# Expert outputs weighted per slot and scattered with an adding DMA into an output that already holds x1

## What is computed

```python
x = x + _L0_gnn_ref(_layernorm(x), ..., src, dst)                  # x1
x_flat = _layernorm(x)
gate_logits = x_flat @ Wg + bg + bias                              # 8 experts
topk_vals, topk_idx = jax.lax.top_k(gate_logits, 2)
topk_w = jax.nn.softmax(topk_vals, axis=-1)
combine = (one_hot(topk_idx, 8) * topk_w[..., None]).sum(axis=1)
h = relu(einsum('td,edh->teh', x_flat, W1) + b1)                   # 256 -> 512
y = einsum('teh,ehd->ted', h, W2) + b2                             # 512 -> 256
x = x + einsum('ted,te->td', y, combine)
```

## Time and profile before

| | us |
|---|---|
| timed runs, median of 3 | 2192.18 |
| lowest and highest | 2184.37, 2199.14 |
| the profiled execution's own time | 2198.43 |
| its span in the profile | 2196.7 |
| first `tick` of the expert loop | 1974.32 |
| last `tock` | 2160.16 |

### The profile page before, as it was taken

How to read it: one execution, slowest core, us unless ns; L and a number is a source line. 1 busy time by engine, 2 the same in 40 slices (tenths; PEclk the granted TensorE clock), 3 DMA queues, 4 the chain that set the end, 5 groups by cost and what they waited for, 6 DMA issues and landing times.

```text
span 2196.7 us, 31507 instructions
## 1 busy us (share of the span) xinstructions
PE 1910.3 (87%) x11090; PEld 1129.8 (51%) x11091; DVE 1117.5 (51%) x2548; ACT 594.1 (27%) x1268; POOL 304.1 (14%) x434
## 2 busy tenths in 40 slices
PE   1666767999999999999999999999999998649991
PEld 1533334445654456445654457444664455439991
DVE  7589992344524445244533445244533655635555
ACT  0145552112221223112222123121221111126660
POOL 0012224554000000000000000000000112123331
PEclk7779998999999999999999999999999999769996
DMA  9900004342000000000000000000000000633225
GB/s 272 336 10 0 0 0 154 133 141 93 1 2 1 1 1 2 1 1 1 1 2 1 1 1 1 1 1 1 1 1 1 20 20 32 284 112 85 78 85 193
DMA packets 74392, 113.64 MB, mean 52 GB/s; under 512 B 10634, under 2 KB 63669, under 8 KB 73232
## 3 DMA queue, kind: packets, MB, share of 16 engines
q1 hardware_dynamic: 56618, 52.49, 8.0%
q0 software_dynamic: 12736, 39.29, 5.2%
q10 hardware_dynamic: 4902, 20.01, 2.3%
HBM read 49.99 MB, written 61.77 MB: 51 GB/s over the span
## 4 chain that ended last, share of the span: by engine, by line
PE 67%; DVE 15%; issue 9%; POOL 5%; ACT 1%; SPq 1%; DMA 1%; ACTq 1%; DVEq 0%; POOLq 0%
PE bank L1401 35%; PE bank L1425 24%; DVE hot_key L759 6%; PE bank L1385 4%; POOL chosen_out L563 3%; DVE hot_row L753 2%; POOL slot_in L542 2%; PE bank L1380 1%; PE bank L1299 1%; SPq L435 1%; PE bank L1469 0%; DMA y_pair<-chosen_out 0%; PE bank L1327 0%; PE bank L1462 0%; DVE r_lo L819 0%
## 5 line engine op out<-in xcount | busy, mean ns | idle before, releaser
L1401 PE MATMUL bank<-adj,r_hi 128*128 128x512 fp8e4 (+2 forms) x2100 | 732.6, 353 | 0.0
L1401 PE MATMUL bank<-adj,r_lo 128*128 128x512 fp8e4 (+2 forms) x2100 | 732.2, 353 | 0.0
L1401 PEld LDWEIGHTS bank<-adj,r_hi 128*128 128x128 f16 x2100 | 206.4, 98 | 190.5 <-issue 2.0
L1401 PEld LDWEIGHTS bank<-adj,r_lo 128*128 128x128 f16 x2100 | 206.4, 98 | 190.5 <-issue 1.7
L826 DVE SCALAR_TENSOR_TENSOR m_lo<-bank,msg_unit,m_hi 128x512 f16<-128x512 f32 (+2 forms) x84 | 57.3, 683 | 302.3 <-ACT m_hi L1112 302.3
L1327 PE MATMUL bank<-hot_key,hot_row 128*128 128x400 f16 x588 | 138.9, 351 | 60.5 <-DVE hot_key L759 58.1
L1425 PE MATMUL bank<-x_hi,wht_hi 128*128 128x512 f16 (+2 forms) x504 | 178.0, 353 | 9.2 <-DVE gate_a L844 9.2
L1425 PE MATMUL bank<-x_lo,wht_hi 128*128 128x512 f16 (+2 forms) x504 | 178.0, 353 | 0.0
L1425 PE MATMUL bank<-x_hi,wht_lo 128*128 128x512 f16 (+2 forms) x504 | 178.0, 353 | 0.0
L1425 PE MATMUL bank<-m_hi,wct_hi 128*128 128x512 f16 (+2 forms) x504 | 177.8, 353 | 0.0
L1425 PE MATMUL bank<-m_lo,wct_hi 128*128 128x512 f16 (+2 forms) x504 | 177.7, 353 | 0.0
(11 more groups left out here) (279 smaller groups left out, 2893.4 us busy)
## 6 DMA issues: line engine op xcount, KB each, us to landing
slot_in<-fill_rows SPq DMA_DIRECT2D x2, 13520.0 KB, 69.4
ffn_scratch<-pair POOLq DMA_DIRECT2D x32, 512.0 KB, 3.2
ffn_w<-ffn_scratch ACTq DMA_DIRECT2D x8, 2048.0 KB, 16.0
x_rows<-in_L_ffn_W POOLq DMA_DIRECT2D x32, 256.0 KB, 4.0
slot_x<-slot_in SPq DMA_DIRECT2D x30, 260.0 KB, 2.8
y_pair<-chosen_out SPq DMA_DIRECT2D x8, 640.0 KB, 9.0
xa<-in_x SPq DMA_DIRECT2D x1, 3072.0 KB
x<-in_x ACTq DMA_DIRECT2D x1, 3072.0 KB
```

The costliest lines, as they stand in the source:

```text
L1401: last = mm(bank[f][:, 0:n], r[:, q, f * P:(f + 1) * P], c, start=q == 0 and i == 0, stop=q == NT - 1 and i == len(todo) - 1)
```

## The change

The weights are now applied in the expert loop, to each slot, and the scatter adds into `out` itself.

- The top logits' difference d travels with the row, in column `D + 2` of `x2_rows`, `slot_in` and `slot_x`. The work on `top` ahead of the loop is gone.
- ACT forms e^d per tile (`exp_now`) ahead of `xt_hi`; DVE keeps it in `meta` beside the two numbers.
- `output` writes the biased result into `y_sum`, makes `dest` (the node number alone), the weight `share`, and then `slot_y` in two multiplications. PE's `layer2` waits for `y_sum` only (`y_read`).
- The scatters go into `out` with `compute_op=ALU.add`; rows beyond the last node are out of bounds and left out.
- SP stores x1 into `out` window by window in the GNN's last step; GpSimd waits for these stores before the expert loop.
- The tail is gone.

```diff
@@ block.sync: in place of the wait for "rows"
-            sp.wait_ge(sem("rows"), rows_before(NW))
+            for w in range(NW):
+                t0, t1 = WIN_T0[w], WIN_T0[w] + WIN_TILES[w] - (w == NW - 1)
+                sp.wait_ge(sem("x1_sum"), rows_before(w + 1))
+                sp.dma_start(out[t0 * P:t1 * P, :].rearrange("(t p) d -> p t d", p=P), x1[:, t0:t1, :]).then_inc(sem("stored"), 16)
+            sp.dma_start(out[(NT - 1) * P:N, :], x1[0:TAIL, NT - 1, :]).then_inc(sem("stored"), 16)
             for e in range(NX):
                 sp.dma_start(out_bias[:, e, :], ...)
@@ block.sync: the end
             sp.wait_ge(sem("experts_done"), 1)
-            G = NT // FIN
-            for g in range(FIN):
...
-            for g in range(FIN):
-                t0, t1 = g * G, (g + 1) * G
-                sp.wait_ge(sem("summed"), t1)
...
-            sp.wait_ge(sem("stored"), 16 * (FIN + 1))
@@ block.gpsimd
+            pool.wait_ge(sem("stored"), 16 * (NW + 1))
             pool.wait_ge(sem("tiles_of"), 1)
...
-                    pool.wait_ge(sem("y_ready"), 2 * n + 4)
+                    pool.wait_ge(sem("y_ready"), n + 1)
                     pool.tensor_tensor(tick[:], valid[:], valid[:], ALU.mult).then_inc(sem("ticks"), 1)
                     for j in range(TT):
-                        pool.indirect_dma_start(chosen_out[:], bass.IndirectOffsetOnAxis(ap=dest[:, j:j + 1], axis=0),
-                                                slot_y[:, j, :], None).then_inc(sem("y_out"), 16)
+                        pool.indirect_dma_start(out[:], bass.IndirectOffsetOnAxis(ap=dest[:, j:j + 1], axis=0), slot_y[:, j, :], None,
+                                                bounds_check=N - 1, oob_is_err=False, compute_op=ALU.add).then_inc(sem("y_out"), 16)
@@ block.vector: choose
+                v.tensor_tensor(x2_rows[w % 2][:, 0:nt, D + 2], top[:, 1, t0:t0 + nt], top[:, 0, t0:t0 + nt], ALU.subtract)
@@ block.vector: before the loop
-            v.tensor_tensor(top[:, 2, :], top[:, 1, :], top[:, 0, :], ALU.subtract).then_inc(sem("top_diff"), 1)
-            dve.wait_ge(sem("top_exp"), 1)
...
@@ split_tile
-                v.tensor_copy(kept, slot_x[:, :, D:D + 2]).then_inc(sem("meta_kept"), 1)
+                v.tensor_copy(kept[:, :, 0:2], slot_x[:, :, D:D + 2])
+                v.tensor_copy(kept[:, :, 2], exp_now[:]).then_inc(sem("meta_kept"), 1)
@@ output
-                v.tensor_tensor(slot_y[:], bank[5][:]..., out_bias[:, e:e + 1, :]..., ALU.add)                 .then_inc(sem("y_ready"), 1)
+                v.tensor_tensor(y_sum[:], bank[5][:]..., out_bias[:, e:e + 1, :]..., ALU.add)\
+                 .then_inc(sem("y_read"), 1)
                 v.tensor_copy(meta_now[:], meta[:, bass.ds(n, 1), :, :]...).then_inc(sem("dest_part"), 1)
...
-                v.tensor_scalar(dest_f[:], meta_now[:, :, 1], float(e), float(NPAD), ALU.not_equal, ALU.mult).then_inc(sem("dest_part"), 1)
-                dve.wait_ge(sem("dest_part"), 2 * n + 2)
-                v.tensor_tensor(dest[:], dest_f[:], meta_now[:, :, 0], ALU.add).then_inc(sem("y_ready"), 1)
+                v.tensor_copy(dest[:], meta_now[:, :, 0])
+                v.tensor_scalar(total[:], meta_now[:, :, 2], 1.0, None, ALU.add).then_inc(sem("dest_part"), 1)
+                v.scalar_tensor_tensor(share[:], meta_now[:, :, 1], float(e), meta_now[:, :, 2], ALU.is_equal, ALU.max).then_inc(sem("dest_part"), 1)
+                dve.wait_ge(sem("dest_part"), DEST_OPS * n + 2)
+                v.reciprocal(total[:], total[:]).then_inc(sem("dest_part"), 1)
+                dve.wait_ge(sem("dest_part"), DEST_OPS * n + 4)
+                v.tensor_tensor(share[:], share[:], total[:], ALU.mult).then_inc(sem("dest_part"), 1)
+                dve.wait_ge(sem("dest_part"), DEST_OPS * n + 5)
+                dve.wait_ge(sem("y_read"), n + 2)
+                for j in range(TT):
+                    last = v.tensor_scalar(slot_y[:, j, :], y_sum[:, j, :], share[:, j:j + 1], None, ALU.mult)
+                last.then_inc(sem("y_ready"), 1)
@@ block.vector: the end
-            for t in range(NT):
...
-                v.scalar_tensor_tensor(x1[0:m, t, :], y_pair[0:m, t, 0, :], top[0:m, 0, t:t + 1], x1[0:m, t, :], ALU.mult, ALU.add).then_inc(sem("first_summed"), 1)
...
@@ block.scalar
-            act.wait_ge(sem("top_diff"), 1)
-            a.activation(top[:, 2, :], top[:, 2, :], ACT.Exp).then_inc(sem("top_exp"), 1)
 
             def tile_hi(n):
                 act.wait_ge(sem("turned"), n + 2)
+                a.activation(exp_now[:], slot_x[:, :, D + 2], ACT.Exp)
                 a.activation(xt_hi[:]..., bank[4][:], ACT.Copy).then_inc(sem("tile_hi"), 1)
@@ block.tensor
             def layer2(e, n):
-                pe.wait_ge(sem("y_ready"), 2 * n + 2)
+                pe.wait_ge(sem("y_read"), n + 1)
```

More of the change, by code:

```diff
@@ L68 @@
 TT = TILE // P
+DEST_OPS = 5
 CAP = (N + TILE - 1) // TILE * TILE
@@ L232, in gnn_ffn @@
         x2_rows = [lb(f"x2_rows{i}", [P, 4, ROW], F32) for i in range(2)]
-        top = lb("top", [P, 4, NT], F32)
+        top = lb("top", [P, 2, NT], F32)
         mv2 = lb("mv2", [P, NT, 2], F32)
@@ L282, in gnn_ffn @@
         xt_lo = fb("xt_lo", [P, DT, TILE], F32R)
-        meta = fb("meta", [P, MAX_TILES + 2, TT, 2], F32)
-        meta_now = fb("meta_now", [P, TT, 2], F32)
-        dest_f = fb("dest_f", [P, TT], F32)
+        meta = fb("meta", [P, MAX_TILES + 2, TT, 3], F32)
+        meta_now = fb("meta_now", [P, TT, 3], F32)
+        exp_now = fb("exp_now", [P, TT], F32)
+        total = fb("total", [P, TT], F32)
+        share = fb("share", [P, TT], F32)
+        y_sum = fb("y_sum", [P, TT, D], F32)
         dest = fb("dest", [P, TT], U32)
@@ L313, in gnn_ffn @@
         slot_in = nc.dram_tensor("slot_in", (NX * CAP, ROW), F32, kind="Internal").ap()
-        chosen_out = nc.dram_tensor("chosen_out", (3 * NPAD + TILE, D), F32, kind="Internal").ap()
         ffn_dram = nc.dram_tensor("ffn_scratch", (NX, P, 2, 2, DT * HID), F32, kind="Internal").ap()
@@ L989, in _ @@
             v.tensor_scalar(tiles_of[:], tiles_i[:], TILE.bit_length() - 1, None, ALU.arith_shift_right).then_inc(sem("tiles_of"), 1)
-            v.tensor_tensor(top[:, 2, :], top[:, 1, :], top[:, 0, :], ALU.subtract).then_inc(sem("top_diff"), 1)
-            dve.wait_ge(sem("top_exp"), 1)
-            link(v.tensor_scalar(top[:, 3, :], top[:, 2, :], 1.0, None, ALU.add))
-            link(v.reciprocal(top[:, 0, :], top[:, 3, :]))
-            link(v.tensor_tensor(top[:, 1, :], top[:, 2, :], top[:, 0, :], ALU.mult))
             def split_tile(n):
@@ L1038, in _ @@
                 dve.reg_add(done, done, 1)
-            for t in range(NT):
-                m = TAIL if t == NT - 1 else P
-                if t % (NT // FIN) == 0:
-                    g = t // (NT // FIN)
-                    dve.wait_ge(sem(f"outputs{g}"), 64 if g == FIN - 1 else 32)
-                v.scalar_tensor_tensor(x1[0:m, t, :], y_pair[0:m, t, 0, :], top[0:m, 0, t:t + 1], x1[0:m, t, :], ALU.mult, ALU.add).then_inc(sem("first_summed"), 1)
-                dve.wait_ge(sem("first_summed"), t + 1)
-                v.scalar_tensor_tensor(x1[0:m, t, :], y_pair[0:m, t, 1, :], top[0:m, 1, t:t + 1], x1[0:m, t, :], ALU.mult, ALU.add).then_inc(sem("summed"), 1)
         @block.scalar
@@ L1561, in _ @@
             pe.wait_ge(sem("tiles_of"), 1)
-            for name, n in (("turned", 1), ("meta_kept", 1), ("xt_split", 1), ("h_act", HT), ("h_lo", HT), ("y_part", HT), ("y_ready", 2), ("y_sent", 1)):
+            for name, n in (("turned", 1), ("meta_kept", 1), ("xt_split", 1), ("h_act", HT), ("h_lo", HT), ("y_part", HT), ("y_read", 1), ("y_sent", 1)):
                 mm(bank[6][:, 0:2], all_ones[:], before[:, 0:2], start=True, stop=True).then_inc(sem(name), n)
```

23 lines of the change are left out of this document (3 added, 20 removed).

## The result

| | before | after |
|---|---|---|
| time, median (lowest to highest) | 2191.43 us (2184.37 to 2199.14) | 2239.43 us (2235.29 to 2242.89) |
| span of the profiled execution | 2196.7 us | 2239.2 us |
| first `tick`, last `tock` | 1974.32, 2160.16 | 1978.88, 2233.54 |
| from one `tick` to the next, mean of 28 | 6.49 us | 8.905 us |
| last `tock` to the span's end | 36.5 us | 5.7 us |

The changed kernel is 48 us slower: ratio 1.0196, 95% interval 1.0172 to 1.022. The forecast was 2216 us with a range of 2176 to 2255.

What follows compares the result with a forecast made beforehand. A ring of VectorE's writes and GpSimd's scatters was taken to bound the loop. First `tick` 1977.0, 28 x (2.6 + 4.5), 4.1 + 0.5 and 29 x 1.4 gave +24 us on 2196.7; carried to the median 2192.18: 2216 us, range 2176 to 2255.

Steps and rivals of the forecast that it cites:

- The tail: After the expert loop, VectorE and DMA work alone for the last 37 us; removing it was to save 36.0 us.
- the ring: Expert loop: `tock` lets VectorE write `slot_y`, releasing `tick` and two scatters, whose landing releases `tock`; any lengthening paid 28 times.
- my own last sign of being wrong: On GpSimd: the forecast is wrong if issuing an adding scatter takes longer than a plain one's 0.96 us.
- x: Extra time per tile of adding over plain scatters, placed in the landing: 1.4 us, the middle of 0 to 2.8.
- rival 1: Wait of `tock`: the addition costs one more pass at most, 0.37 to 0.74 us a tile, 2187 to 2197 us; chance 0.22.
- VectorE's part: From `tock` to `tick` in each tile: grows by 1.0 us, to near 2.6 us.
- The start: First `tick` of the expert loop: 1974.32 + 1.7 + 1.0 = 1977.0.
- The table load: ACT's load for Exp moves behind the first tile's transpose: 1.28 us, with two exponentials together +1.7 us.
- The end: After the last `tock`: only `ended` and the end of the program remain, estimated at 0.5 us.
- The argument on the place of the next load: Expert loop: `slot_x` load released 0.7 to 0.9 us after `tick` spares the scatters; 4.5 us from `tick` to `tock`.
- Rival 2: Scatters: the addition is served row by row, 2.1 to 2.8 us or more a tile; 2257 us at 2.8; chance 0.23.
- Rival 3: TensorE loses its clock in the loop's gaps; at 1.2 GHz throughout over 100 us more; chance 0.03.

Runs made afterwards that it cites:

- the run with the late load: The changed kernel with SP's load of `slot_x` held back until the scatters of the tile in hand have landed; 2241.13 us, 1.0216 of before.

## Why the prediction was right, and where it was too low

The direction and the mechanism held: the tail goes, the ring becomes the bound, and its 28 rounds cost more than the tail gave. The size was half of what came, and the place of the largest term was wrong: by my own last sign of being wrong, an issue longer than 0.96 us, the reasoning behind x fails (1.55 us). Other signs failed too: `tick` to `tock` is 6.40 us and not near 5.9, GpSimd's wait for `out<-slot_y` is 61.8 us and not above 100, and the span ends 5.7 us after the last `tock` and not within 1. Against the forecast's span of 2221.0 (2180.4 + 29 x 1.4) the profiled 2239.2 is 18.2 us longer, in these terms:

- **The addition, x.** Forecast 1.4 us, measured 1.64: +6.7 us. The larger miss is its place. I put all of it into the fetch behind the issue and priced the issue at the plain scatter's 1.29 us distance. The test that I had named, the distance between the two issues, reads 1.94 us. The landing adds only 0.54 to 0.76 us, close to the 0.37 to 0.74 of rival 1; what rival 1 and I both lacked is GpSimd's time. That x came within 0.24 us all the same is luck: an overpriced landing made up for an issue priced at nothing. The Trainium skill's rule ("Collectives: The Full Stack", section "Why ReduceScatter is half of AllGather") has an addition read two sources, which halves the rate. Here the DMA engines' time per scatter grew 2.8 times, from 0.38 to 1.08 us with all rows written; that a second read is what lengthens the landing, no run shows. The rule says nothing of the issuing engine's time, which is the larger part.
- **The bounds check**, priced at nothing: +0.48 us ahead of the second scatter, of which the skipped rows give 0.22 back. A plain `tick` to `tock` was forecast at 4.5 us and is 4.76 in the kernel without the addition: +7.3 us over 28 tiles.
- **VectorE's part**: forecast 2.6 us, measured 2.50. The chain `y_sum`, `meta_now`, `total`, reciprocal, `share`, `slot_y` ran as worked out, to within 0.1 us in all: -2.8 us.
- **The start**: first `tick` 1978.88, forecast 1977.0, +1.9 us. The two traces can be compared, since the last scatter into `slot_in` starts at 1945.26 in before and 1945.06 in after; other traces of the same GNN end up to 5 us earlier. The stores of x1 ahead of the loop cost nothing, as forecast: the first load is issued at 1952.72 and 1952.71. The first `xt_hi` is 1.4 us later (forecast: 1.7, the second exponential included) and VectorE's part 0.9 us longer (1.0). The rest, some 2 us, goes with TensorE's clock: from 1968 to 1971 us it was granted 0.50 in after and 1.00 in before. The table load did come where it was expected:

```profile
1956.76 1.28 ACT L1171 ACT_TABLE_LOAD   x1 [28.43 <-PE bank L1518]
```

- **The end**: I allowed 0.5 us from the last `tock`, and it is 5.7. Both programs have this stretch. Before, the last store's issue ended at 2191.34 and the span at 2196.7; I had read these 5.4 us as the store's landing and counted them as gained. They stay when no store is left: +5.2 us. This agrees with the kernel before without its tail (30.6 us gained behind the last `tock`, not 36).
- **The last tile**: 5.3 us instead of 5.5, -0.2.

Together 6.7 + 7.3 - 2.8 + 1.9 + 5.2 - 0.2 = 18.1. The other 5 us between 2216 and 2239 come from the step to the median: the profiled execution of before took 6.2 us more than its median of 2192.18, that of after (2240.96) only 1.5 us more than its own, and I had carried the whole 6.2 over.

The argument on the place of the next load held better than the run with the late load suggests. That run compares two harmless places. In after, SP issues the load 0.9 us after `tick` in most tiles, as forecast, and the landing is what it is without the load. The harmful place is later. In before, seven tiles had the load issued 1.94 to 2.20 us after `tick`, and their landings took 2.80 to 3.18 us; in six tiles it was issued 1.05 to 1.24 us after, and they took 1.58 to 2.03; loads 1.52 to 1.81 us after `tick` lie between, at 1.89 to 2.62. The last three tiles, without a load, took 1.51 to 1.52, and so did, to 0.04 us, four of the five whose load came 2.83 us or more after `tick`. With the addition, before without its tail had 2.86 to 3.06 us in four of the six tiles whose load came 1.79 to 2.19 us after `tick` (2.30 and 2.57 in the others), and 2.21 to 2.41 where it came at 1.05 to 1.25. This also is where the loops of before and of before without its tail part: the loads of the first met the scatters from the sixth tile on, those of the second only from the 19th. It is read from traces, not from a run that moves the load there; why the first landing got longer in the fifth and the 18th tile is open.

Rival 2 (row by row, x of 2.1 or more) is out: `tick` to `tock` is 6.40, below its 6.6. Rival 3 is out in its strong form: in the loop the clock stayed at 0.89 or above. The weak form was not foreseen. I had argued from a stretch in which TensorE was 69% busy at 1.00; from 2010 to 2060 us it was 82% busy in after and was granted 0.90, so that row did not carry over. TensorE waited 56.4 us for `y_sum`, so I read no price for this in the loop.

## What to carry to other kernels

Price an indirect scatter by the engine that issues it as well as by its landing: whatever adds packets or a bound lengthens GpSimd's part, and in a ring of one buffer every tenth of a microsecond is paid per tile. When a change turns the end of a program into work inside a loop, first make sure that the loop does not wait for that work; with two buffers and a wait only where rows can meet, the addition costs about 5 us and not 47. And a span here has some 5 us at its end that no removed work gives back.

## What the runs showed of the hardware

- An adding indirect scatter of 128 rows of 1 KB keeps GpSimd for 1.55 us, a plain one for 0.96; it makes 144 packets, the plain one 48, and takes 1.08 us of each DMA engine against 0.38.
- A bound on its indices puts 0.4 us ahead of the first scatter behind a `tick` (0.75 us for 0.35), whether it adds or not. Rows left out by the bound shorten the landing, in the last tile from 2.28 to 1.21 us.
- A tile load issued some 2 us after `tick` goes with a longer landing of the scatters: 2.80 to 3.18 us for 1.52 in the plain kernel.
- A scatter's issue took up to 2.71 us instead of 1.55 in ten tiles in which a run of VectorE operations began just before it; the cause is open.
- Four writes of 128 separate 4-byte elements on GpSimd's queue, behind 12 scatters, held up the next tile load by 11 to 12 us.
